# Query and value stages of a GPS layer joined into one list of 20 products

## What is computed

```
q, k, v = split(xn @ w_qkv)              # 1250 x 512 each, 8 heads of 64
q = softmax(q, over the 64 of a head) / 8
k = softmax(k, over the 1250 nodes)
context = k^T (v / N)                    # per head 64 x 64
out = layernorm(context applied to q, @ w_out + b_out) * ln_scale
```

## Time and profile before

| | |
|---|---|
| median of 3 runs | 604.46 us (602.67 to 605.23) |
| the profiled execution | 604.85 us |
| its span, first to last instruction | 603.0 us |
| mean granted clock of PE, 1 is full speed | 0.928 |
| PE busy | 500.5 us, 83% of the span |
| DVE busy | 369.8 us, 61% |
| ACT busy | 228.7 us, 38% |
| POOL busy | 179.8 us, 30% |
| chain that ended last, by engine | PE 62%, DVE 17%, ACT 7%, issue 6% |

### The profile page before, as it was taken

One profiled execution on the slowest core, in us unless ns is written; L12 is line 12 of the kernel. 1 busy time (PEld: TensorE's weight loads), 2 busy tenths in 40 slices (PEclk: granted clock), 3 DMA queues, 4 the chain that ended last, 5 costly groups with the idle time before them and its releaser, 6 DMA issues.

```text
span 603.0 us, 11695 instructions
## 1 busy us (share of the span) xinstructions
PE 500.5 (83%) x3899; PEld 394.6 (65%) x3899; DVE 369.8 (61%) x758; ACT 228.7 (38%) x502; POOL 179.8 (30%) x151
## 2 busy tenths in 40 slices
PE   0279799999889889969999979899999689866760
PEld 0159678766556756649988867699889579535530
DVE  1679988858878377426166434213654655399794
ACT  1373322273423422223345457211553677203431
POOL 1222410044510210112974510002452000465873
PEclk9999979999879999979999998899999679887985
DMA  4321010000010100020000100000302750000022
GB/s 143 132 105 70 9 62 3 1 30 41 1 71 1 43 29 1 1 72 2 0 1 1 70 0 0 2 0 2 121 0 70 316 245 2 0 1 2 0 77 93
DMA packets 4812, 27.41 MB, mean 45 GB/s; under 512 B 604, under 2 KB 729, under 8 KB 3112
## 3 DMA queue, kind: packets, MB, share of 16 engines
q1 hardware_dynamic: 4516, 25.90, 11.5%
q10 hardware_dynamic: 260, 1.02, 0.5%
HBM read 24.36 MB, written 2.56 MB: 45 GB/s over the span
## 4 chain that ended last, share of the span: by engine, by line
PE 62%; DVE 17%; ACT 7%; issue 6%; DMA 3%; POOL 3%; DVEq 0%; ACTq 0%; SPq 0%; POOLq 0%
PE ps L417 37%; PE ps L555 15%; PE ps L404 4%; DVE stage L1284 4%; DMA x<-in_x 3%; PE ps L468 2%; PE ps L458 2%; DVE stat L1002 2%; POOL r L1426 1%; PE ps L401 1%; ACT r L835 1%; DVE qsum L1097 1%; DVE r L1091 1%; ACT late L755 1%; DVE r L980 1%
## 5 line engine op out<-in xcount | busy, mean ns | idle before, releaser
L417 PE MATMUL ps<-r,wslot 128*128 128x250 f16 (+1 forms) x840 | 100.3, 283 | 10.0 <-DVE wslot L981 5.1
L417 PE MATMUL ps<-late,wslot 128*128 x960 | 104.6, 270 | 1.2 <-ACT ohs L809 1.2
L1377 POOL TENSOR_TENSOR wslot<-stage,wslot 128x2048 f16<-128x2048 f32 x10 | 40.8, 4079 | 214.7 <-ACT wslot L693 127.8
L417 PEld LDWEIGHTS ps<-late,wslot 128*128 128x128 f16 x960 | 92.2, 97 | 13.3 <-issue 3.2
L417 PEld LDWEIGHTS ps<-r,wslot 128*128 128x128 f16 x840 | 85.6, 102 | 22.8 <-DVE wslot L981 5.9
L555 PE MATMUL ps<-late,r 125*128 (+1 forms) x800 | 92.9, 279 | 8.9 <-issue 8.9
L555 PEld LDWEIGHTS ps<-late,r 125*128 125x128 f16 x800 | 79.9, 100 | 20.2 <-issue 10.0
L417 PE MATMUL ps<-wslot,r 128*125 128x512 f16 x300 | 74.4, 404 | 8.0 <-DVE r L1327 4.9
L981 DVE SCALAR_TENSOR_TENSOR late<-ps,late 128x250 f32 (+2 forms) x60 | 30.1, 508 | 72.1 <-ACT late L842 61.9
L417 PEld LDWEIGHTS ps<-wslot,r 128*125 128x125 f16 (+1 forms) x300 | 42.2, 146 | 33.2 <-issue 14.2
L700 ACT ACTIVATE late<-ps 125x500 f16<-125x500 f32 (+1 forms) x25 | 14.7, 588 | 95.0 <-PE ps L404 95.0
(11 more groups left out here) (155 smaller groups left out, 752.2 us busy)
## 6 DMA issues: line engine op xcount, KB each, us to landing
late<-in_tv SPq DMA_DIRECT2D x2, 4096.0 KB, 17.4
out<-r SPq DMA_DIRECT2D x10, 250.0 KB
stage<-in_w_up SPq DMA_DIRECT2D x2, 1024.0 KB, 4.9
stage<-in_w_down SPq DMA_DIRECT2D x2, 1024.0 KB, 4.9
x<-in_x SPq DMA_DIRECT2D x3, 500.0 KB
stage<-in_w_lin SPq DMA_DIRECT2D x1, 1024.0 KB, 21.6
stage<-in_w_k SPq DMA_DIRECT2D x1, 1024.0 KB, 5.2
stage<-in_w_q SPq DMA_DIRECT2D x1, 1024.0 KB, 4.9
```

Source lines behind the costliest of these rows:

```text
L417: last = nc.tensor.matmul(out, stat_(hs, b), mov(hm, b), start=start and n == 0, stop=stop and n == 3 * blocks - 1)
L1377: nc.gpsimd.tensor_tensor(wslot[:, i % SLOTS, 1].rearrange("p k n -> p (k n)"), stage[:, :], wslot[:, i % SLOTS, 0].rearrange("p k n -> p ...
```

## The change

Query and value become one list, `QV`, of 20 products with 20 uses of the "n" ring: q0 to q6, then v0, q7, v1, q8, v2, q9, v3, and v4 to v9. The ten flips of k move two each beside query tiles 2 to 6. Each engine walks this list:
- PE: product; after q2 to q6 two flips; after v_t (from v1 on) window t - 1.
- ACT: for a query tile two high parts of k (tiles 2 to 6), then the exponential; for a value tile the high part of v_t, then the copy of window t, and in v0 the split of "out" behind it.
- DVE: for a query tile maximum and subtraction, then sum and inverse of the tile before, then two low parts of k; for a value tile the low part of v_t and **then** the one-hots of window t.
- POOL: the split of "out" comes ahead of the ten multiplications.

A new semaphore, `v_high`, counts the high parts of v.

```diff
--- before.py
+++ after.py
@@ -75,9 +75,16 @@
 WINDOWS = {"k": 2, "v": 2, "mix": 1}
 
 
+Q_FIRST, KN_LAG = 7, 2
+QV = [("q", _t) for _t in range(Q_FIRST)]
+for _t in range(T):
+    QV += [("v", _t)] + ([("q", Q_FIRST + _t)] if Q_FIRST + _t < T else [])
+assert len(QV) == 2 * T and 2 * (Q_FIRST - KN_LAG) == T
+
+
 
 USES = {
-    "n": [("q", T, "dve", 0), ("v", T, "dve", 1), ("m", KB, "dve", 1), ("mix", T, "dve", 0), ("ffn2", T, "dve", 0)],
+    "n": [("qv", 2 * T, "dve", 0), ("m", KB, "dve", 1), ("mix", T, "dve", 0), ("ffn2", T, "dve", 0)],
     "t": [("lin", 20, "act", 0), ("k", 20, "dve", 0), ("agg0", 20, "dve", 1), ("up0", 20, "act", 0),
           ("down0", 20, "act", 0), ("agg1", 20, "dve", 1), ("up1", 20, "act", 0), ("down1", 20, "act", 0),
           ("gate", 20, "act", 0), ("ffn1", 10, "act", 0)],
@@ -88,7 +95,7 @@
 }
 RING = {"n": 2, "t": 4, "x": 2, "y": 2}
 
-BANKS_FROM = {"q": ("t", "k", 17), "agg0": ("n", "mix", 9), "ffn2": ("t", "ffn1", 9)}
+BANKS_FROM = {"qv": ("t", "k", 17), "agg0": ("n", "mix", 9), "ffn2": ("t", "ffn1", 9)}
 
 
 def before(family, phase, who=None, high=False):
@@ -135,7 +142,7 @@
 assert sum(WINDOWS.values()) * J == NWIN and J == HT
 
 
-READER = {"lin": ("t", "lin"), "k": ("t", "k"), "q": ("n", "q"), "v": ("n", "v"), "out": ("n", "m"), "up0": ("t", "up0"),
+READER = {"lin": ("t", "lin"), "k": ("t", "k"), "q": ("n", "qv"), "v": ("n", "qv"), "out": ("n", "m"), "up0": ("t", "up0"),
           "down0": ("t", "down0"), "up1": ("t", "up1"), "down1": ("t", "down1"), "gate": ("t", "gate")}
 
 
@@ -293,7 +300,7 @@
         g_oh, g_used, g_full, g_high, g_low = sems("g_oh", "g_used", "g_full", "g_high", "g_low")
 
         var_ready, std_ready, norm_ready, ln_done = sems("var_ready", "std_ready", "norm_ready", "ln_done")
-        k_max, k_exp, q_exp, q_rec, q_soft, mixed = sems("k_max", "k_exp", "q_exp", "q_rec", "q_soft", "mixed")
+        v_high, k_max, k_exp, q_exp, q_rec, q_soft, mixed = sems("v_high", "k_max", "k_exp", "q_exp", "q_rec", "q_soft", "mixed")
 
         lin_out, prelu_out, hid_high, tmp_free, bias_ready, layer_out = sems(
             "lin_out", "prelu_out", "hid_high", "tmp_free", "bias_ready", "layer_out")
@@ -436,9 +443,10 @@
                         ready(j)
                     product_chunk(phase, w, mov, j, bass.ts(j, CH))
 
-            def natural_tile(phase, mov, w, t):
-                wait_bank(pe, "n", phase, t, t % 2)
-                passes(bank("n", t % 2)[0:P, :], lambda h, b: mov[:, h, b, t * P:(t + 1) * P], lambda h, b: w[:, h, b, :], KB
+            def natural_tile(phase, mov, w, t, use=None):
+                use = t if use is None else use
+                wait_bank(pe, "n", phase, use, use % 2)
+                passes(bank("n", use % 2)[0:P, :], lambda h, b: mov[:, h, b, t * P:(t + 1) * P], lambda h, b: w[:, h, b, :], KB
                        ).then_inc(full["n"], 1)
 
             def natural(phase, mov, w, blocks=KB, ready=None):
@@ -496,21 +504,19 @@
             windows("k", J - 1, KB - 1, KB)
             wait_weight(pe, "q")
 
-            for t in range(T + 2):
-                if t < T:
-                    natural_tile("q", xn_t, weight("q"), t)
-                if t >= 2:
+            for i, (kind, t) in enumerate(QV):
+                if (kind, t) == ("v", 0):
+                    wait_weight(pe, "v")
+                natural_tile("qv", xn_t, weight(kind), t, i)
+                if kind == "q" and KN_LAG <= t < Q_FIRST:
                     pe.wait_ge(k_exp, KB)
-                    flip_tile_to_nat("x", "kn", k_t, t - 2)
-
-            wait_weight(pe, "v")
-            for t in range(T):
-                natural_tile("v", xn_t, weight("v"), t)
-                if t:
+                    for u in (2 * (t - KN_LAG), 2 * (t - KN_LAG) + 1):
+                        flip_tile_to_nat("x", "kn", k_t, u)
+                if kind == "v" and t:
                     windows("v", (t - 1) // 2, (t - 1) % 2, 2)
             windows("v", HT - 1, 1, 2)
 
-            wait_done(pe, "n", "v", T)
+            wait_done(pe, "n", "qv", 2 * T)
             wait_done(pe, "x", "kn", T)
             for b in range(2):
                 wait_bank(pe, "x", "ctx", b, b)
@@ -756,16 +762,19 @@
                                      accum_out=ksum[:, m:m + 1]).then_inc(k_exp, 1)
             split_weight("v")
 
-            for t in range(T + 2):
-                if t < T:
-                    wait_done(act, "n", "q", t + 1)
+            for i, (kind, t) in enumerate(QV):
+                if kind == "q":
+                    if KN_LAG <= t < Q_FIRST:
+                        for u in (2 * (t - KN_LAG), 2 * (t - KN_LAG) + 1):
+                            high_tile_nat("x", "kn", k_nat, S_K, u, u % 2)
+                    wait_done(act, "n", "qv", i + 1)
                     nc.scalar.activation(q_nat[:, t, :], q_nat[:, t, :], ACT.Exp, scale=S_XW).then_inc(q_exp, 1)
-                if t >= 2:
-                    high_tile_nat("x", "kn", k_nat, S_K, t - 2, t % 2)
-            split_weight("out")
-            for t in range(T):
-                high_tile_nat("n", "v", v_nat, 1 / S_W, t, t % 2)
-                windows("v", t // 2, t % 2, 2)
+                else:
+                    wait_full(act, "n", "qv", i)
+                    nc.scalar.activation(v_nat[:, 0, t, :], bank("n", i % 2)[0:P, :], ACT.Copy, scale=1 / S_W).then_inc(v_high, 1)
+                    windows("v", t // 2, t % 2, 2)
+                    if t == 0:
+                        split_weight("out")
             split_weight("up0")
 
             act.wait_ge(consts, 1)
@@ -1084,21 +1093,31 @@
             def per_head(ap):
                 return ap.unsqueeze(2).to_broadcast([P, H, DH])
 
-            for i in range(HT + 1):
-                for t_ in (2 * i, 2 * i + 1) if i < HT else ():
-                    wait_full(dve, "n", "q", t_)
-                    then(nc.vector.tensor_reduce(qmax[:, t_, :], heads_of(bank("n", t_ % 2)[0:P, :]), AX.X, ALU.max))
-                    nc.vector.tensor_tensor(heads_of(q_nat[:, t_, :]), heads_of(bank("n", t_ % 2)[0:P, :]),
-                                            per_head(qmax[:, t_, :]), ALU.subtract).then_inc(free["n", "dve"], 1)
-                for t_ in (2 * i - 2, 2 * i - 1) if i else ():
-                    low_tile_nat("x", "kn", k_nat, S_K, t_, t_ % 2)
-                for t_ in (2 * i, 2 * i + 1) if i < HT else ():
-                    dve.wait_ge(q_exp, t_ + 1)
-                    then(nc.vector.tensor_reduce(qsum[:, t_, :], heads_of(q_nat[:, t_, :]), AX.X, ALU.add))
-                    nc.vector.reciprocal(qsum[:, t_, :], qsum[:, t_, :]).then_inc(q_rec, 1)
-            for t in range(T):
-                windows("v", t // 2, t % 2, 2)
-                low_tile_nat("n", "v", v_nat, 1 / S_W, t, t % 2)
+            def q_shift(i, t):
+                wait_full(dve, "n", "qv", i)
+                q = heads_of(bank("n", i % 2)[0:P, :])
+                then(nc.vector.tensor_reduce(qmax[:, t, :], q, AX.X, ALU.max))
+                nc.vector.tensor_tensor(heads_of(q_nat[:, t, :]), q, per_head(qmax[:, t, :]), ALU.subtract).then_inc(free["n", "dve"], 1)
+
+            def q_sum(t):
+                dve.wait_ge(q_exp, t + 1)
+                then(nc.vector.tensor_reduce(qsum[:, t, :], heads_of(q_nat[:, t, :]), AX.X, ALU.add))
+                nc.vector.reciprocal(qsum[:, t, :], qsum[:, t, :]).then_inc(q_rec, 1)
+
+            for i, (kind, t) in enumerate(QV):
+                if kind == "q":
+                    q_shift(i, t)
+                    if t:
+                        q_sum(t - 1)
+                    if KN_LAG <= t < Q_FIRST:
+                        for u in (2 * (t - KN_LAG), 2 * (t - KN_LAG) + 1):
+                            low_tile_nat("x", "kn", k_nat, S_K, u, u % 2)
+                else:
+                    dve.wait_ge(v_high, t + 1)
+                    low(v_nat[:, 1, t, :], bank("n", i % 2)[0:P, :], v_nat[:, 0, t, :], 1 / S_W).then_inc(free["n", "dve"], 1)
+                    windows("v", t // 2, t % 2, 2)
+                    if t == T - Q_FIRST:
+                        q_sum(T - 1)
             dve.wait_ge(k_exp, KB)
             nc.vector.reciprocal(krec[:, :], ksum[:, :]).then_inc(k_max, 1)
             dve.wait_ge(k_max, 2)
@@ -1377,14 +1396,14 @@
                 nc.gpsimd.tensor_tensor(wslot[:, i % SLOTS, 1].rearrange("p k n -> p (k n)"), stage[:, :],
                                         wslot[:, i % SLOTS, 0].rearrange("p k n -> p (k n)"), ALU.subtract).then_inc(w_split, 1)
 
-            for name in ("lin", "k", "q", "v"):
+            for name in ("lin", "k", "q", "v", "out"):
                 split_weight(name)
             with pool.Fori(0, T) as t_:
                 pool.wait_ge(q_rec, t_ + 1)
                 tile = q_nat[:, bass.ds(t_, 1), :].rearrange("p o (h d) -> p (o h) d", h=H)
                 nc.gpsimd.tensor_tensor(tile, tile, qsum[:, bass.ds(t_, 1), :].rearrange("p o h -> p (o h)").unsqueeze(2)
```

(2 more changed lines are left out.)

## The result

The changed kernel takes 623.12 us (four runs, 619.37 to 628.20) against 604.50 (four runs, 602.67 to 605.23). The ratio is 1.031, 95% interval 1.024 to 1.039. Forecast were 626.5 us, a range of 611 to 635, and slower with a chance of 0.93. The four runs after are 619.37, 620.80, 625.45 and 628.20. In the ratios, runs more than 1.5% above the fastest of their kernel are left out; medians and ranges have them all.

What follows compares the result with a forecast made beforehand. PE was taken to bound the query and value stages. Handovers of 6.69 us a tile against 3.60 put the context products at 223.3, not 201.21: 604.85 + 22 = 626.9, less 0.4 to the median, 626.5; range 611 to 635.

Steps and rivals of the forecast that it cites:

- The order of DVE in a value tile: Value tiles: one-hots now wait for the previous window, closing the handover chain over one tile: 6.69 us against 3.60.
- L965 to the end of the window, 3.68: Value tiles: from offsets to a window's last matmul, 3.68 us for register loading and sixteen matmuls; lower bound 1.92.
- rival 1: Value tiles: same loop but cheaper, 4.92 us a tile by the bound; 608, or halfway 612 to 620; chance 0.15.
- Flips in pairs: Query stage: PE loses about 1 us to late DVE at first, v0 starts at about 144.5, 2 us gained.
- Split of "out" earlier: Before window 11: the 4.58 us wait goes, ACT's half costs 1.9 uncovered, POOL's 4.08 subtraction stands against the one-hots.
- The multiplications later: Window 11: POOL's multiplications take turns with DVE's one-hot instructions, 2.7 us; bounds 0 and 3.7.
- Half clock, 1 us: Window 12: after PE's idling, half clock slows q9 and v3 by a few us, mostly slack; 1 us counted.
- rival 2: Value tiles: PE's clock stays at half, 13 us more in all; 632 to 640; chance 0.12.
- Behind them every engine's order is as before: After the context products: order unchanged, so their 22 us later start is carried to the end.
- rival 3: Value tiles: PE stays the bound at 3.60 a turn or less, stage ends at 188.3, 13 us earlier; 591.5; chance 0.05.
- rival 4: Query and value stages: gain and loss cancel, within 3 us; chance 0.02.

Runs made afterwards that it cites:

- e1: Changed kernel, but DVE makes the one-hots of window t before it takes the low part of v_t: 596.57 us, ratio 0.988.
- e2: Kernel before, but DVE takes the low part of v_t before it makes the one-hots of window t: 635.62 us, ratio 1.049.
- e3: Changed kernel, but ACT copies window t - 1, not window t, behind the high part of v_t: 603.71 us, ratio 0.997.
- e7: Changed kernel, but DVE makes the offsets before the one-hot of the sources: 620.94 us, ratio 1.028.
- e8: e1, and POOL multiplies query tiles 0 to 4 before it splits "out": 596.12 us, ratio 0.987.
- e10: Changed kernel, but SP does PE's first four semaphore increments, so PE's program is four shorter: 627.46 us, ratio 1.037.
- e9_before_pad20: Kernel before with twenty unread semaphore increments at the start of PE's program: 598.79 us, ratio 0.988.
- e5: Kernel before with four unread semaphore increments at the start of PE's program: seven runs, median 597.70 us, ratio 0.987 without the two slow ones.
- e6: Kernel before with four such increments behind the branch, just ahead of the up0 products: 605.02 us, ratio 1.000.

## Why the prediction was right, and where not

Times of day in the profile after start 0.9 us earlier, so 0.9 is to be added to compare with the sum.

- *The order of DVE in a value tile* was the part that decides, and it did: 6.69 a turn was forecast, 6.65 to 6.8 measured; 40.1 for the last six windows, 40.3 measured (window 13 ends at 180.78, window 19 at 221.08). e1 and e2 show that this order makes it, in either kernel, and e3 that it needs ACT's copy in the same loop.
- *L965 to the end of the window, 3.68.* The value held (190.47 to 194.07 is 3.60), and so the lower bound of rival 1 fell. Its explanation, "the loading of the registers and sixteen matmuls", was half right: e7 moves the registers out of the way and gains nothing.
- *Flips in pairs*: v0 was forecast at 144.5, it starts at 143.52 + 0.9 = 144.4. The lost 1 us is there too, as a wait of 0.86 before a pair of flips.
- *Split of "out" earlier*: L967 ends with POOL's subtraction at 159.1 (160.1 less 0.9 was forecast), PE idles 1.61 before v2 (about 2).
- *The multiplications later*: 2.7 was taken from the turns in the rows; it was 1.5. L974 to the end of window 11 is 5.11 instead of 3.6, since one turn falls on L974 and one on L980, and the second in front of L974, which was counted, is missing. These 1.2 us too many are why the stage grew by 20.7 and not by 22. The rule of the Trainium skill (SBUF — State Buffer, "Who interferes with whom") by which `rel` would meet one as well did not lengthen window 11: L976 starts 0.93 after L974 and keeps its usual 0.30. The trace doesn't speak against the rule for that: the multiplication at 161.12 began 0.01 us behind L976 and took 1.20 instead of 1.04, and the one at 159.06, behind L969, took 2.10. It was POOL that waited.
- *Half clock, 1 us* for window 12: 8.25 from window 11 to 12, where 7.26 plus 1 stood. About 0.85 of it is a multiplication in front of L974, so this term was right in size by luck and mostly wrong in its cause. In the prediction the two products of 7.03 us stand beside the hole of 2.45; by their time, 154.37, they follow the one of 1.84, and the product behind the 2.45 takes 5.18. In the tail the clock did fall in some turns (products of 4.46 at 180.70 and 193.99 between products of 2.77), as rival 2 had it, but such a product still ends in time, so it cost nothing there. It cost 2.1 behind the tail, in the context products (granted clock 0.75 instead of 1.00); the sum had no term for it. What brings the clock down there is open: in the changed kernel PE idled 4.41 us before the last window, but e8 has the same (0.80) with 0.81 us of idling.
- *"Behind them every engine's order is as before"* is the step that failed. The order was the same and PE was 6.8 us faster there, because its branch stood four instructions later in the program. In the profiled execution +16.0 is +20.7 in the stage, +2.1 in the context products and -6.8 at the branch, the rest 0, where +22 was forecast. e10, the changed kernel with the branch in its old place, is 22 us above the kernel before. That this is the forecast to the microsecond is luck in part: the multiplications were 1.2 too long in the sum and the context products' 2.1 were not in it. It is luck too that the median, 623.12, lies as near to 626.5 as it does: it is the middle between two runs near 620 and two at 625 and 628.

What the wait at the branch is can be read from the DMA view. Two queues there are of the kind "instruction", q8 and q14, and q8 moves one block of 16 KB at a time. That q8 serves PE is inferred: between its transfers at 201.96 and 207.93 in the kernel before PE has some 220 instructions (matmuls and weight loads) and no other engine has ten. The times below are in us; the second part of the first sums ends at PE's branch.

| trace | first sums, second part | q8 transfers start | PE's next matmul | idle |
|---|---|---|---|---|
| before | 255.82 to 259.84 | 262.67 | 265.09 | 5.25 |
| e10_after_minus4 | 278.88 to 282.89 | 285.68 | 288.11 | 5.22 |
| after | 277.72 to 281.74 | 279.71, 284.55 | 282.40 | 0.66 |
| e9_before_pad20 | 256.59 to 260.61 | 257.81, 263.50 | 261.27 | 0.67 |

The line of q8 in the DMA view (transfers, MB, share of 16 engines), first before, from 259.84 to 265.09, then after, from 277.72 to 281.74; before has no such line from 255.82 to 259.84:

```profile
q8 instruction: 1, 0.02, 1.1%
```

```profile
q8 instruction: 1, 0.02, 1.5%
```

All thirteen traces are of one of these two kinds. In five (before, e2, e5, e6, e10) no block comes during these sums, the next one starts 2.8 us behind them, and PE goes on 2.4 us after that start, 5.1 to 5.3 us after its last matmul. In the eight others a block has come 1.5 to 2.9 us before the sums end, and PE idles 0.7 to 0.9. By all of them the long wait is a wait for instructions, and the place of the branch decides whether they are there. This agrees with the Trainium skill (Runtime: NRT & Kernel Launch, "Instruction fetch mechanics"): instructions come in blocks of 256, prefetch is sequential, and a taken branch to a block that isn't there waits for a fetch. Which instructions a block holds, and so where exactly its edge lies, no view shows. In e5 the same program has the wait in some runs and most likely not in others, so four instructions put the branch near that edge and twenty well past it. Not every such wait went away: at the branch of the second layer PE idles 3.4 to 3.8 us in the traces of before, after, e5, e6, e9 and e10 alike.

Of the rivals: rival 3 (PE stays the bound) did not come, and in e1 it does not even with the right order: with the query tiles between and POOL's turns DVE is the bound in the middle of the stage, and the context products begin at 199.47, not at 188. Rival 1 fell by the just-in-time windows, rival 4 with it. Rival 2 came in its clock and not in its cost.

## What to carry to other kernels

When a change turns two statements of one engine, follow the chain of handovers through all engines and count over how many turns of the loop it closes: the sum of its handovers over that number is the turn, wherever it is more than what the busiest engine has to do in one. Here the same work took 6.7 us a tile with the chain over one tile, 4.5 with another chain over two, and 3.6 where PE's own work is the bound. And before a gain or a loss of 1% is put down to an edit, look at the places that it does not touch: four idle instructions ahead of a branch were worth as much here.

## What the runs showed of the hardware that was not expected

- PE's wait at one taken branch is 5.1 to 5.3 us or 0.7 to 0.9 us by where the branch stands in its program, and in the long ones a 16 KB block of instructions arrives inside the wait. With the half clock behind it that is 6.8 us between before and after (43.1 against 36.3 from the end of the first sums to up0), and 5.6 us between e10 and after. Four added instructions that do nothing make five runs of seven some 8 us shorter.
- Sixteen matmuls of 80 columns with addresses in registers take 0.75 us when PE comes to them late, and 1.9 to 2.1 us when it waits for their operands, at full clock too (1.94 at 192.13, granted 1.00), even where the clear shows the registers loaded 1.2 us before (e7).
- The granted clock fell in a loop in which PE stands still for 1.7 us of 6.7: in every second turn in e2 (products of 4.2 to 4.5 and of 2.78 in turn), in two turns of six in the first trace of the changed kernel. It cost nothing as long as the slow product fitted in.
- VectorE and GpSimd each wait for the other here: a multiplication of 1.04 us took 2.10 behind L969, 1.20 behind L976 and 1.62 behind L980, and L974 took 1.00 instead of 0.15 behind a multiplication.
